# Latent attention on one core: query rotation split by head, u of two heads on the two column halves

## What is computed

```python
x = x + L0_xattn(layernorm(x), ctx, ...)             # the stage that the change touches
# inside, per head h, with H = 16 heads, K = 128, D_CQ = 192, D_C = R = 64:
q_big = einsum('bshk,hkq->bshq', hidden_q @ Wq.T, w_kc_q)          # 192 rows a head
q_big = q_big * cos_q + rotate_half(q_big) * sin_q                 # rotate_half: (-upper 96, lower 96)
q_r = einsum('bshq,hqr->bhsr', q_big, W_qr)
k_r = einsum('bld,hdr->bhlr', kv_r, W_kr)                          # kv_r: rotated context
attn = softmax(einsum('bhsr,bhlr->bhsl', q_r, k_r))
ctx_c = einsum('bhsl,bld->bhsd', attn, kv_r)
out = (ctx_c through w_kc_kv and Wo)
# then: an FFN in emulated FP8, a second attention, a gated FFN
```

## Time and profile before

| | |
|---|---|
| time, median of 3 runs | 470.81 us (469.98 to 470.88) |
| the profiled execution's own time | 468.11 us |
| its span | 466.3 us |
| TensorE matmul busy | 408.9 us, 88% |
| VectorE busy | 310.8 us, 67% |
| ScalarE busy | 214.5 us, 46% |
| GpSimd busy | 184.0 us, 39% |
| the main loop of the groups | about 33 to 240 us of the span |

### The profile page before, as it was taken

How to read it: one execution, slowest core, us unless ns; L and a number is a source line. 1 busy time by engine, 2 the same in 40 slices (tenths; PEclk the granted TensorE clock), 3 DMA queues, 4 the chain that set the end, 5 groups by cost and what they waited for, 6 DMA issues and landing times.

```text
span 466.3 us, 5952 instructions
## 1 busy us (share of the span) xinstructions
PE 408.9 (88%) x1991; PEld 262.6 (56%) x1997; DVE 310.8 (67%) x681; ACT 214.5 (46%) x562; POOL 184.0 (39%) x149
## 2 busy tenths in 40 slices
PE   1989999999999999999899998287772987999997
PEld 1766666676666766666567784133341453533475
DVE  4898768665776566767787656188799856574322
ACT  1336646665566646654578533058850124321100
POOL 1496554555445655545452349670001200040000
PEclk9999999999999999999999999699898899999999
DMA  8752020200201100003000051000000000000011
GB/s 317 263 188 84 1 91 1 77 17 0 91 0 37 55 1 1 1 5 121 1 0 2 1 114 47 0 0 1 1 1 0 0 1 1 0 1 0 1 45 45
DMA packets 8941, 18.82 MB, mean 40 GB/s; under 512 B 2128, under 2 KB 6672, under 8 KB 7760
## 3 DMA queue, kind: packets, MB, share of 16 engines
q1 hardware_dynamic: 8912, 18.46, 11.5%
HBM read 17.40 MB, written 1.05 MB: 40 GB/s over the span
## 4 chain that ended last, share of the span: by engine, by line
PE 56%; DVE 27%; issue 5%; POOL 5%; ACT 4%; DMA 3%; SPq 1%; DVEq 0%; ACTq 0%
PE bank L1146 6%; PE bank L1395 5%; PE bank L1413 5%; PE bank L1159 5%; PE bank L1085 4%; PE bank L1183 4%; PE bank L1189 4%; PE bank L1171 4%; PE bank L1087 3%; PE bank L1086 3%; DVE rot_z L752 3%; PE bank L1279 3%; DVE uT L777 2%; DVE tail_all L1006 2%; PE bank L1106 2%
## 5 line engine op out<-in xcount | busy, mean ns | idle before, releaser
L418 POOL TENSOR_TENSOR prob<-prob,rinv 128x512 f32<-128x512 f32 x64 | 67.7, 1057 | 103.2 <-DVE rinv L818 101.1
L562 ACT ACTIVATE prob<-bank,negmax 128x256 f32<-128x256 f32 x128 | 59.5, 471 | 51.5 <-DVE negmax L813 51.4
L813 DVE TENSOR_REDUCE negmax<-bank 128x2 f32<-128x512 f32 x64 | 44.0, 688 | 29.8 <-PE bank L1159 29.4
L392 POOL TENSOR_TENSOR c_y<-c_ve,minus_half 128x4 f32<-128x4 f32 (+1 forms) x10 | 12.4, 1243 | 97.3 <-DVE c_ve L699 69.9
L1159 PE MATMUL bank<-kvT,uT 128*128 128x256 f32 x256 | 46.4, 303 | 0.4 <-issue 0.4
L413 POOL TENSOR_TENSOR rot_low<-rot_low,rot_up 128x1024 f32<-128x1024 f32 x16 | 38.7, 2419 | 16.4 <-DVE rot_up L746 16.2
L1395 PE MATMUL bank<-tailT,blobs 128*128 128x512 f32 (+1 forms) x96 | 42.7, 597 | 1.8 <-ACT tailT L505 0.8
L1279 PE MATMUL bank<-wfc,ident 128*128 128x512 bf16 x139 | 36.5, 411 | 7.3 <-DVE xs L921 6.7
L1085 PE MATMUL bank<-xnT,w 128*128 128x512 f32 x96 | 40.2, 419 | 2.8 <-DVE rot_z L752 2.4
L553 ACT COPY probT<-bank 128x512 f32<-128x512 f32 x64 | 37.4, 585 | 9.3 <-PE bank L1171 8.6
L1159 PEld LDWEIGHTS bank<-kvT,uT 128*128 128x128 f32 x256 | 34.5, 189 | 12.5 <-issue 12.3
(11 more groups left out here) (188 smaller groups left out, 757.1 us busy)
## 6 DMA issues: line engine op xcount, KB each, us to landing
blobs<-in_blob SPq DMA_DIRECT2D x8, 1024.0 KB, 6.1
xs<-in_x SPq DMA_DIRECT2D x2, 512.0 KB, 4.1
ctxT<-in_ctx_t SPq DMA_DIRECT2D x1, 1024.0 KB, 13.2
xn<-in_w_fc_t SPq DMA_DIRECT2D x1, 1024.0 KB, 5.1
ctxT<-in_w_proj_t SPq DMA_DIRECT2D x1, 1024.0 KB, 5.6
out<-qk SPq DMA_DIRECT2D x8, 128.0 KB, 1.7
cb<-in_const_b SPq DMA_DIRECT2D x1, 768.0 KB, 9.0
blobs<-in_w_gate SPq DMA_DIRECT2D x1, 704.0 KB, 4.3
```

Of the source, the lines that this page charges most:

```text
L418: pool.tensor_tensor(p[:], p[:], rinv[:, n % PROBS, :].unsqueeze(2).to_broadcast([P, 2, S]), ALU.mult).then_inc(normed, 1)
L562: ins = act.activation(prob[n % PROBS][:, st, :], pS[n % 2][:, st * S:(st + 1) * S], ACT.Exp, bias=negmax[:, n % 2, st:st + 1], accum_out= ...
```

## The change

The chunks are put together by head. Chunk 0 holds, of head 0, the lower rows 0 to 63 and their upper partners 96 to 159; chunk 1 the same of head 1; chunk 2 the rest of both (32 lower rows of each head, then their partners). Every chunk now holds its own partners, on the other half of the partitions.

- `rope` makes for each of the three chunks one product of 128x512 and two of 64x512 (it was so for chunk 2 alone).
- `join` is three additions of 128x512, one after each chunk, instead of one of 128x1024 and one of 128x512.
- u: the chunks 0 and 1 have one head each, so they go into the two column halves of the array as two matmuls of 64 weight columns (`pu` partitions 0 to 63 and 64 to 127), both in j1; the shared chunk 2 is one matmul of 128 columns, alone in j3. Three matmuls of 128 columns over 512 become two of 64 and one of 128.
- `wqk` is 256 columns wide instead of 384; its fold has two matmuls over 64 columns and one over 128 instead of three over 128.
- The copies of `w1` take the rows from the bank in another pattern, and the tables and `rows` on the host are laid out to match.

```diff
-            def join(n, z):
-                pool.wait_ge(rot_ready, RT * n + 2 + z)
+            def join(n, r):
+                pool.wait_ge(rot_ready, RT * n + r + 1)
                 low, up, rz = rots(n)
-                if z:
+                if r == 2:
                     pool.tensor_tensor(rz[:, 0, :], rz[:, 0, :], rz[:, 1, :], ALU.add).then_inc(joined, 1)
                 else:
-                    pool.tensor_tensor(low, low, up, ALU.add).then_inc(joined, 1)
+                    pool.tensor_tensor(low[:, r, :], low[:, r, :], up[:, r, :], ALU.add).then_inc(joined, 1)
...
-                if s % 2 == 1 and m < ALLQ and m % RT:
-                    join(m // RT, m % RT - 1)
+                if s % 2 == 1 and m < ALLQ:
+                    join(m // RT, m % RT)
...
-                    act.copy(wqk[f % 2][:], pW[:, 0:RT * P]).then_inc(wqk_ready, 1)
+                    act.copy(wqk[f % 2][:], pW[:, 0:2 * P]).then_inc(wqk_ready, 1)
...
-                if r == 0:
-                    if n >= 2:
-                        dve.wait_ge(u_ready, RT * (n - 2) + 2)
-                    dve.tensor_tensor(tokens(low[:, 0, :]), tokens(src[:]), angles(cosq, 0), ALU.mult)
-                    ins = dve.tensor_tensor(tokens(low[:, 1, :]), tokens(src[:]), angles(sinq, 0), ALU.mult)
-                elif r == 1:
...
+                if r == 0 and n >= 2:
+                    dve.wait_ge(u_ready, 2 * (n - 2) + 1)
+                if r < 2 and n:
+                    dve.wait_ge(joined, RT * (n - 1) + r + 1)
+                if r == 2 and n >= 2:
+                    dve.wait_ge(u_ready, 2 * (n - 1))
+                straight, crossed = (low[:, r, :], up[:, r, :]) if r < 2 else (rz[:, 0, :], rz[:, 1, :])
+                dve.tensor_tensor(tokens(straight), tokens(src[:]), angles(cosq, r), ALU.mult)
+                for lo, to in ((0, DC), (DC, 0)):
+                    ins = dve.tensor_tensor(tokens(crossed[to:to + DC, :]), tokens(src[lo:lo + DC, :]),
+                                            angles(sinq, r, lo, lo + DC), ALU.mult)
                 ins.then_inc(rot_ready, 1)
...
-            def latent_u(n, r):
+            def latent_u(n, shared):
...
+                pe.wait_ge(joined, RT * n + 2 + shared)
+                if shared:
+                    pe.matmul(pu[:], wqk[f % 2][:, P:2 * P], rz[:, 0, :], start=False, stop=True).then_inc(u_ready, 1)
+                    return
+                pe.wait_ge(wqk_ready, f + 1)
+                if n:
+                    pe.wait_ge(u_copied, n)
+                for h in range(2):
+                    ins = pe.matmul(pu[h * DC:(h + 1) * DC, :], wqk[f % 2][:, h * DC:(h + 1) * DC], low[:, h, :],
+                                    start=True, stop=False)
+                ins.then_inc(u_ready, 1)
```

More of the change, by code:

```diff
@@ L175, in build @@
             w1 = [[part(f"w1_{j}_{i}", [P, DK, 2 * DCQ]) for i in range(2)] for j in range(2)]
-            wqk = [part(f"wqk_{j}", [P, RT * P], F32) for j in range(2)]
+            wqk = [part(f"wqk_{j}", [P, 2 * P], F32) for j in range(2)]
             uT = [part(f"uT_{j}", [P, 2, CH]) for j in range(2)]
@@ L423, in _ @@
             join(0, 1)
+            join(0, 2)
             turn_keys(1, A_ST)
             join(1, 0)
+            join(1, 1)
             kt = bf_m[:].rearrange("p a t -> p (a t)").bitcast(F32)[:, 0:NT * DC].rearrange("p (b a d) -> p b a d", b=B, a=2)
@@ L443, in _ @@
             pool.memset(pad, 0.0).then_inc(kva_ready, 1)
-            join(1, 1)
+            join(1, 2)
             for s in range(SLOTS, LAST + 1):
@@ L1103, in prep @@
                 if i < 2:
-                    o = pW[:, 0:2 * DCQ].rearrange("p (u h n) -> p u h n", u=2, h=2)
+                    o = pW[:, 0:2 * DCQ].rearrange("p (h u n) -> p h u n", h=2, u=2)
                     for h in range(2):
-                        ins = pe.matmul(o[:, :, h, :], w_view(f, C_WQ, D)[:, h, i * P:(i + 1) * P],
+                        ins = pe.matmul(o[:, h, :, :], w_view(f, C_WQ, D)[:, h, i * P:(i + 1) * P],
                                         w_view(f, C_KCQ, DCQ)[:, h, :].rearrange("p (u n) -> p u n", u=2),
@@ L1110, in prep @@
                     blob_f = wb[f % NBLOB]
-                    for r in range(RT):
-                        ins = pe.matmul(pW[:, r * P:(r + 1) * P], blob_f[:, C_QR + r * P:C_QR + (r + 1) * P],
-                                        blob_f[:, C_KR:C_KR + P], start=True, stop=True)
+                    for r, (lo, hi) in enumerate(((0, DC), (DC, P), (0, P))):
+                        at = 0 if r < 2 else P
+                        ins = pe.matmul(pW[:, at + lo:at + hi], blob_f[:, C_QR + r * P:C_QR + (r + 1) * P],
+                                        blob_f[:, C_KR + lo:C_KR + hi], start=True, stop=True)
                 else:
@@ L1135, in latent_q @@
                 ins.then_inc(q_ready, 1)
-            def latent_u(n, r):
+            def latent_u(n, shared):
                 f = n // 2
-                pe.wait_ge(joined, 2 * n + r // 2 + 1)
-                if r == 0:
-                    pe.wait_ge(wqk_ready, f + 1)
-                    if n:
-                        pe.wait_ge(u_copied, n)
-                low, _, rz = rots(n)
-                pe.matmul(pu[:], wqk[f % 2][:, r * P:(r + 1) * P], rz[:, 0, :] if r == 2 else low[:, r, :],
-                          start=(r == 0), stop=(r == RT - 1)).then_inc(u_ready, 1)
+                low, _, rz = rots(n)
+                pe.wait_ge(joined, RT * n + 2 + shared)
[9 more added lines that the diff above has]
+                ins.then_inc(u_ready, 1)
             def scores(n):
@@ L1227, in _ @@
             prep(1, 1)
-            for r in range(RT):
-                latent_u(0, r)
+            latent_u(0, 0)
+            latent_u(0, 1)
             prep(1, 2)
@@ L1426, in tables @@
     sin_q, cos_q = sincos(DCQ)
-    low = np.concatenate([np.arange(HALF), np.arange(P - HALF)])
-    rest = np.arange(P - HALF, HALF)
+    own, rest = np.arange(DC), np.tile(np.arange(DC, HALF), 2)
     cos_t, sin_t = cos_q.T, sin_q.T
-    cos_rows = [cos_t[low], cos_t[low + HALF], np.concatenate([cos_t[rest], cos_t[rest + HALF]])]
-    sin_rows = [sin_t[low + HALF], -sin_t[low], np.concatenate([sin_t[rest + HALF], -sin_t[rest]])]
+    cos_rows = [np.concatenate([cos_t[i], cos_t[i + HALF]]) for i in (own, own, rest)]
+    sin_rows = [np.concatenate([sin_t[i + HALF], -sin_t[i]]) for i in (own, own, rest)]
     const_b = np.concatenate(cos_rows + sin_rows, axis=1)
@@ L1472 @@
     quarters = np.arange(2 * DCQ).reshape(2, 2, HALF)
-    cut = P - HALF
-    rows = np.concatenate([quarters[0, 0], quarters[1, 0, :cut], quarters[0, 1], quarters[1, 1, :cut],
-                           quarters[1, 0, cut:], quarters[1, 1, cut:]])
+    rows = np.concatenate([quarters[:, :, :DC].reshape(-1), quarters[:, :, DC:].transpose(1, 0, 2).reshape(-1)])
     blob = np.concatenate([wq, paired(a(L0_xattn_w_kc_q)), paired(a(L0_xattn_w_kc_kv)), wo_t,
```

27 lines of the change are left out of this document (7 added, 20 removed).

## The result

| | before | after |
|---|---|---|
| median, same chip | 470.39 us (468.94 to 470.88, 4 runs) | 482.61 us (480.98 to 484.14, 4 runs) |
| profiled execution's own time | 468.11 us | 484.00 us |
| span | 466.3 us | 482.2 us |

The changed kernel is slower: ratio 1.0267, interval 1.0239 to 1.0296. Between the medians lie 12.2 us, forecast were 12.6.

A forecast was written before the change was run, and what follows sets the result against it. TensorE, nearly full, leads, but VectorE's work before `w1_low` and k2's maximum decides when it goes on. Terms 4.3 + 5.9 + 2.2 + 0.8 - 0.6 = 12.6 us slower, on 468.11 giving 480.7, plus 2.7: 483.4 us, range 479 to 488.

The forecast's parts named there:

- The likeliest case: Whole kernel: longer ropes on VectorE make it 12.6 us slower, 483.4 us; chance 0.82.
- A longer rope, +0.91: VectorE, ropes of chunks 0 and 1: two added 64x512 instructions a group cost 0.91 us more per rope, 1.82 a group.
- The pair, 1.11: TensorE, j1: two 64-column u matmuls side by side cost 0.86 + 0.25 = 1.11 us, 0.25 more in j1.
- the rival in series: TensorE, j1: the two half-column matmuls do not run side by side, 0.86 us more in j1; 488 us, chance 0.08.
- The saving of 0.60 a group, 9.6 in all: TensorE: u of a group goes from 2.57 to 1.97 us, 9.6 us less over 16 groups.
- The start, +4.3: First rope to chunk 2's rotation at 45.81: VectorE bounds; six longer ropes add 5.5 us, idle gaps take some, +4.3.
- The groups after it: Main loop behind the start: +0.92 us per group with the third fold in j1, +0.37 per group without it.
- the ScalarE chain behind this maximum is unbroken: Group with the fold in j1: k2's maximum is 1.34 us late, and `u_copy`, copies, exponentials and context all follow 1.34 later.
- The last pair, 0.1 + 0.7: Last two groups: first loses about 0.1 us, as GpSimd's join beside a 2.22 us VectorE instruction halves; second loses 0.7.
- The tail, -0.6: Beyond the last pair, with the ropes over: TensorE is full and keeps its own gain of one group, -0.6 us.
- TensorE's 0.86 saved in j3 does not help: Group with the fold in j1: 0.86 us saved in j3 is lost, because ScalarE's chain behind k2's maximum is unbroken.
- The rival in which TensorE's gain wins: Whole kernel: added products fall into VectorE's idle time and TensorE gives its 9.6 us back; 461 us, chance 0.06.

The follow-up runs named there:

- the filled kernel: Changed kernel plus 24 matmuls with unused results, 16 among the folds ahead of the loop and 8 in its first group; 482.23 us, ratio 1.0268.
- The uncrossed split: Kernel before, with one 128x512 product of chunks 0 and 1 made as two uncrossed 64x512 products; 482.79 us, ratio 1.0259.
- the whole-u kernel: Changed kernel with u as three matmuls of 128 columns again, one in j1, two in j3, fold and copy of 384 columns; 484.04 us, ratio 1.0287.
- the filled kernels: Changed kernel with 24 unused matmuls added at the start, 482.23 us, and the same with `w1_low` ahead of the rope of chunk 0, 475.58 us.
- the uncrossed kernel: Changed kernel with one uncrossed 128x512 product in place of the two crossed 64x512 ones of chunks 0 and 1; 467.04 us, ratio 0.9932.
- the second run of before with `w1_low` early: Kernel before with `w1_low` made ahead of the rope of chunk 0, measured again over 12 runs; 469.08 us, ratio 0.9991.
- one join: Changed kernel with one GpSimd addition of 128x1024 behind chunk 1 for chunks 0 and 1, as before; 485.88 us, ratio 1.0320.

## Why the prediction held, and where its steps were off

The forecast was 483.4 us in a range of 479 to 488; the time is 482.6. The likeliest case came, by its own mechanism: VectorE alone gives a loss of this size (482.79), and without it the rest is a gain (467.04). That 12.6 and 12.2 lie so close is partly luck. Without the low clock at the start (the filled kernel to the 7th group, after from there on) the stretches add up to 7.23 + 4.10 + 0.22 = 11.55 us, where the forecast had 7.23 + 5.3 + 0.1; and the 12.2 holds changes of the clock on either side that were not forecast and whose size in the medians no run here shows. By its steps:

- **A longer rope, +0.91:** 2.13 - 1.20 = 0.93 measured, and the third product does step 0.70. The uncrossed split, 0.82, tells why: a step is long where an instruction starts on another part of the partitions than the one before. The Trainium skill, "VectorE: DVE Perf Modes", Two Vector instructions with no wait between them, has this as a rule, which it calls a model. It calls a group of 32 partitions a quadrant; an instruction starts only when all earlier ones have finished if one of its inputs starts in another quadrant than the first input last read from the same memory (SBUF or PSUM), or its output in another than the last output into that memory. The trace agrees, 0.61 where both start at partition 0, 0.70 where one does not. The prediction's lower bound of 0.60 could have been excluded by it, and by chunk 2's own rows, 119.75 - 119.05 = 0.70.
- **The pair, 1.11:** 1.07 measured. Its first two records both lie within 0.65 us of 120.42, so the two heads do run side by side, and the rival in series is out. The term around it was too small: j1 grew by 0.35 in B, not 0.25, since the steps into and out of the pair grew as well, and rope 1 of B starts 0.35 later (6.24 us into the group for 5.89). That is the 0.1 which the prediction set for a dearer change between halves and whole. The saving of 0.60 a group, 9.6 in all, is nearer 0.5 and 8.
- **The start, +4.3:** in the filled kernel, free of low clock, the 4th group starts 34.02 us behind the first, for 30.03: +3.99. The rotation of chunk 2 that ended at 45.81 ends at 51.70 in after, forecast "near 50"; the first latent_q's 0.82 and the low clock, which the prediction did not have, are in that. To the 7th group the filled kernel has +7.23; the prediction's terms to there are 4.3 + 1.34 + 0.67 + 0.92 = 7.23. That they agree to the last digit is luck: the start is 0.3 under its term and the three groups behind it, +3.24 for 2.93, as much over.
- **The groups after it:** forecast +0.92 for A and +0.37 for B, measured +0.73 and +0.25. That term was sized too large by 0.31 a period: the step "the ScalarE chain behind this maximum is unbroken". The maximum of k2 does come 1.31 later in A (1.34 forecast; 127.36 - 118.00 = 9.36 against 8.05), but `u_copy` only 1.24 and the last context 1.11 (14.23 us into the group against 13.12): two gaps of about 0.1 us, ahead of `u_copy` and of the last copy, took 0.2. In B the maximum comes 0.79 later (0.67 forecast) and the last context 0.55. So "unbroken" was nearly right, and I could have read those gaps. (The prediction's 0.84 for `u_low` should read 0.80, 118.43 - 117.63; nothing in the sum uses it.) From the 7th group to the 16th this gives +4.10, forecast 5.3 by the same terms.
- **The last pair, 0.1 + 0.7:** the 15th group is +0.19, the instruction of 2.22 us is now 1.18, as forecast from the shorter join.
- **The tail, -0.6:** not seen; from the 16th group on after is 0.22 slower, which is to be set against 0.7 for that group and -0.6 for what follows, +0.1 together. Whether either is there under the changes of the clock, these runs cannot tell.
- **"TensorE's 0.86 saved in j3 does not help":** true in the changed kernel, where the whole-u kernel lost only 1.4 us, and wrong as a general statement. With VectorE out of the way it is worth 3.1 us, through the maximum of k3 and `u_low`. I had followed only the chain from the maximum of k2 to the context. The one through the maximum of k3, `u_low` and chunk 2's rotation is the one that the row of the next latent_q names as its releaser, and I had used that wait only as slack for the loss.

The rival in which TensorE's gain wins was 461 us. Even without the longer ropes it was 467: of the 9.6 us some 1.6 were never saved, and about half land in waits for the other engines (an estimate from 0.5 us a group and the 3.1 us measured).

## What to carry to other kernels

Packing two small products into column halves pays only if the layout that it needs is free elsewhere: here each group saved about 0.5 us on TensorE and paid 1.9 on VectorE, because a product over half the partitions takes as long as a full one. Ask of every instruction added to an engine that is "only 70% busy" who stands directly behind it in its order; the loss was 0.73 us in a group with a fold behind `w1_low` and 0.25 in one without, not the 1.9 added. And when one chain is made shorter, look for the next one close behind it before writing its gain off.

## What the runs showed of the hardware that I had not expected

- **A tiny VectorE instruction tied to GpSimd.** `wdiag`, 128x2, took 2.19 to 2.22 us beside a join of 128x1024 and 1.18 beside one of 128x512, each time ending 0.03 us behind it. The Trainium skill, "GPSIMD Engine Reference", Specifications, says that GpSimd shares its SBUF interfaces with VectorE and names instructions of VectorE in a 2-port mode among those in contention; the trace shows the wait, not the mode.
- **The clock fell behind short pauses.** In every profiled kernel with the longer ropes and without the filling, 3.4 to 6.8 us at 0.5 (1.2 GHz) begin between 31 and 36 us; in after the fall came behind a pause of 1.64 us and within one of 0.96. Before has none ahead of 293 us, though its TensorE paused too, 1.10 us up to 31.43, and the filled kernels, with these pauses filled, have none there. A stretch of 3.4 us also came up at 222 to 223 in the uncrossed kernel and in the second run of before with `w1_low` early, at 237 to 240 in the kernels with the split product and with one join, and at 231 to 236 in the filled kernels; what sets off which, the runs do not say. Where I could set it against the same group without it, it cost 0.7 and 1.4 us.
- **Half products are not all equal.** Uncrossed halves step 0.61 and 0.69, crossed ones 0.71 and 0.69, of 0.69 us each.
